# Second attention layer of a graph kernel: other rows summed by DMA, one broadcast moved ahead of a product, deeper look-ahead on VectorE

## The reference, cut to what matters

```
h = (x @ W).reshape(n, H, C)
s_src = (h * a_src).sum(-1)
s_dst = (h * a_dst).sum(-1)
e = leaky_relu(s_src[src] + s_dst[dst], 0.2)
emax = segment_max(e, dst)
ee = exp(e - emax[dst])
denom = segment_sum(ee, dst)
alpha = ee / denom[dst]
out = segment_sum(alpha[:, :, None] * h[src], dst)
```

## Time and profile before

| what | us |
|---|---|
| median of 3 executions | 968.72 |
| fastest and slowest of them | 965.46, 971.47 |
| the profiled execution | 965.46 |
| its span, first to last instruction | 963.7 |

### The profile page before, as it was taken

One profiled execution on the slowest core, in us unless ns is written; L12 is line 12 of the kernel. 1 busy time (PEld: TensorE's weight loads), 2 busy tenths in 40 slices (PEclk: granted clock), 3 DMA queues, 4 the chain that ended last, 5 costly groups with the idle time before them and its releaser, 6 DMA issues.

```text
span 963.7 us, 17472 instructions
## 1 busy us (share of the span) xinstructions
PE 915.6 (95%) x6479; PEld 674.7 (70%) x6481; DVE 746.9 (78%) x1704; ACT 364.0 (38%) x484; POOL 132.8 (14%) x154
## 2 busy tenths in 40 slices
PE   6899999989999999999999999999997799999995
PEld 5767676656665565567799999679866666666662
DVE  7978999997976889796899997899989544444443
ACT  5751212123245325324345553265447222222320
POOL 3400000000002000000000000020010344545441
PEclk9999999999999999999999999999998899999998
DMA  9611121255366486477692000169576678778860
GB/s 324 191 62 41 60 79 54 83 186 210 116 244 211 159 278 214 147 260 259 239 369 97 36 1 1 34 152 330 202 282 227 232 185 188 193 175 202 201 156 3
DMA packets 65724, 161.01 MB, mean 167 GB/s; under 512 B 15188, under 2 KB 34518, under 8 KB 62698
## 3 DMA queue, kind: packets, MB, share of 16 engines
q1 hardware_dynamic: 50282, 113.90, 33.8%
q0 software_dynamic: 10944, 38.22, 16.7%
q10 hardware_dynamic: 4416, 7.78, 2.2%
HBM read 109.13 MB, written 50.51 MB: 166 GB/s over the span
## 4 chain that ended last, share of the span: by engine, by line
PE 75%; DVE 18%; issue 3%; ACT 1%; DMA 1%; DVEq 1%; POOLq 0%; ACTq 0%; SPq 0%; POOL 0%
PE PS L2054 48%; PE PS L2353 15%; PE PS L2155 3%; DVE arena L1788 3%; PE PS L2551 2%; DVE arena L1616 2%; DVE arena L1622 1%; PE PS L2236 1%; PE PS L2166 1%; PE PS L2372 1%; DVE arena L1502 1%; PE PS L2566 1%; DVE arena L1437 1%; DVE arena L1599 1%; PE PS L2223 1%
## 5 line engine op out<-in xcount | busy, mean ns | idle before, releaser
L2054 PE MATMUL PS<-arena 128*128 128x384 f16 (+7 forms) x3396 | 560.1, 320 | 7.6 <-DVE arena L2044 3.0
L2054 PEld LDWEIGHTS PS<-arena 128*128 128x128 f16 (+2 forms) x3396 | 318.3, 98 | 210.4 <-issue 7.6
L2353 PE MATMUL PS<-arena 128*128 128x193 f32 (+1 forms) x1200 | 178.5, 310 | 3.6 <-DVE arena L1622 2.9
L2353 PEld LDWEIGHTS PS<-arena 128*128 128x128 f32 x1200 | 176.3, 191 | 5.9 <-DVE arena L1622 3.8
L1194 ACT ACTIVATE arena<-arena,AS 128x1250 f32<-128x1250 f32 x60 | 80.1, 1338 | 72.7 <-DVE arena L1616 71.2
L1622 DVE SCALAR_TENSOR_TENSOR arena<-arena 128x1250 f32<-128x1250 f32 x60 | 87.2, 1454 | 4.8 <-PE PS L2353 4.7
L1502 DVE TENSOR_SCALAR arena<-arena 128x240 f16<-128x240 f16 x324 | 88.5, 273 | 0.0
L1616 DVE SCALAR_TENSOR_TENSOR arena<-arena,AS 128x1250 f32<-128x1250 f32 x55 | 83.0, 1510 | 0.0
L1501 DVE TENSOR_SCALAR arena<-arena 128x128 f16<-128x128 f16 x324 | 79.5, 245 | 0.1
L2043 DVE SCALAR_TENSOR_TENSOR arena<-PS,arena 128x768 f32<-128x768 f32 x27 | 25.8, 957 | 62.6 <-PE PS L2054 62.6
L1326 ACT ACTIVATE arena<-PS 128x1536 f16<-128x1536 f16 x27 | 39.2, 1450 | 75.1 <-PE PS L2551 75.1
(11 more groups left out here) (280 smaller groups left out, 944.6 us busy)
## 6 DMA issues: line engine op xcount, KB each, us to landing
arena<-in_L_ffn_W_dram SPq DMA_DIRECT2D x48, 384.0 KB, 4.0
fr_d<-arena SPq DMA_DIRECT2D x48, 384.0 KB, 3.2
arena<-fr_d SPq DMA_DIRECT2D x16, 1152.0 KB, 12.3
arena<-in_x_dram SPq DMA_DIRECT2D x18, 384.0 KB, 5.5
arena<-rr_d SPq DMA_DIRECT2D x4, 1280.0 KB, 8.1
g_d<-arena SPq DMA_DIRECT2D x10, 388.0 KB, 2.5
acc_d<-arena SPq DMA_DIRECT2D x10, 384.0 KB, 2.9
xf_d<-arena ACTq DMA_DIRECT2D x10, 384.0 KB, 3.1
```

Source lines behind the costliest of these rows:

```text
L2054: m = T.matmul(out, left[i][x], right[i][y], start=first and i + r == 0, stop=last and 3 * i + r == n - 1)
L2353: m = T.matmul(ps[sum_bank(h, b)][:, r * (C + 1):(r + 1) * (C + 1)], (PT1 if deep == 3 else PT)[i % deep][:, d * P:(d + 1) * P], feats, st ...
```

## The change

Three things change in layer 2. `RELU` becomes units 0, 2, 4, 6, 8. `row(1)` on TensorE is issued straight after `row(0)`, ahead of `late_graph(2)`, and its `row_out(1)` on ScalarE ahead of `late_out(2)`. The slope steps in VectorE's loop are issued up to unit `i` + 2 for all `i`, but none at `i` = 0; before it was `i` + 1 at 0, `i` + 2 for 1 to 9, and `i` + 1 from 10 on.

```
-        RELU = (0, 2, 5, 7, 9)
+        RELU = (0, 2, 4, 6, 8)
...
                 row_out(0)
+                row_out(1)
                 late_out(2)
-                row_out(1)
                 late_out(3)
...
-                    while ahead < len(SLOPED) and SLOPED[ahead] <= i + (2 if 0 < i < NT else 1):
+                    while i and ahead < len(SLOPED) and SLOPED[ahead] <= i + 2:
                         if SLOPED[ahead] == NT:
                             dve.wait_ge(s_row_ready, 5)
                         slopes(U0 + SLOPED[ahead], *divmod(SLOPED[ahead], NT))
...
             row(0)
+            row(1)
             late_graph(2)
-            row(1)
             late_graph(3)
             row(2)
```

## The result

The changed kernel takes 972.96 us in the median of 18 executions (970.45 to 977.25); the kernel before, over 18 executions of its own, 967.05. The ratio is 1.0052 with a 95% interval of 1.004 to 1.0064: half a per cent slower, some 5.0 us (3.9 to 6.2). The two medians by themselves are 5.9 us apart, which lies inside that interval. The forecast was 972.1 us in a range of 967.5 to 977.0, with a loss of 3.4 us.

The account below looks back on a forecast made before the run. TensorE and VectorE were taken to bound layer 2 in turns, VectorE in head 1. 2.3 us from the start plus 1.1 from the tail made +3.4; 968.72 + 3.4 = 972.1 us, range 967.5 to 977.

Parts of the forecast that it names:

- Row 1 ahead of late product 2: TensorE, layer 2: row(1) stands waiting for row_out(0) from 630.4 to 632.5; first exponential 2.09 us later.
- No slope step at unit 0: Start of VectorE's loop: VectorE idles 2.7 us, row(3) waits for row_out(2), aggregation of unit 1 comes 2.9 us late.
- The other five units: Layer 2, new RELU list: summed rows land in time, units 6 and 8 wait under a microsecond; costs nothing.
- From here to the weights of unit 17 VectorE is without idle time, seven slope steps and six weights: VectorE from 672.26 to 690.55, at 1.43 us a slope step and 1.38 a weights step; unit 18 then 2.3 late.
- The tail: End of the loop: weights of unit 19 wait for the aggregation of 17, until 694.53; adds 1.1 us.
- The walk: Unit by unit timing of layer 2 on three engines; last weights start at 694.53 in place of 691.13, +3.4 us.
- The clock fell behind the standstill: Rival: TensorE's clock falls over row(1) and the late product behind it, losing about 1.6 us more; +5.0 us, chance 0.2.
- The look-ahead did not pay: Rival judged: VectorE runs without a gap from 642.50 to 691.7 instead of 692.6; -0.9 us, chance 0.12.
- The sums did not land late: Rival judged: all five summed rows in layer 2 land 5 us later; about +6.2 us, chance 0.06.
- the +5.0: Loop end 5.0 us late if TensorE's clock falls behind the new standstill; rival, chance 0.2.

Follow-up runs that it names:

- u_swap: The changed kernel with row(1) and row_out(1) put back behind late product 2; 969.27 us, ratio 1.0023 to the kernel before.
- a_first: The changed kernel with the slope step of unit 1 put back ahead of the first weights; ratio 1.003 to the kernel before, stage 88.56 us.
- u_relu: The changed kernel with RELU back at units 0, 2, 5, 7, 9; ratio 1.0043 to the kernel before.
- a_tail: The changed kernel with only the last slope step (unit 19) issued one unit later, at unit 18; ratio 1.0046 to the kernel before.
- b_fill: The kernel before with only the slope step of unit 12 issued earlier, ahead of the denominators; 965.98 us, ratio 0.9971.

## Why the prediction was right, and where its sum was short

**Sign and size.** Forecast +3.4 us; the stage gave +4.5 and the timed runs +5.0 (3.9 to 6.2), so the loss was larger than forecast, by more than the interval. That 972.1 us came so near to 972.96 is luck in part: the 968.72 it was added to, a median of three, lies 1.7 above the 967.05 of eighteen, and this made up for a loss forecast too small.

**Row 1 ahead of late product 2.** Right. A standstill of "30.4 to 632.5" measured 2.02 us, released by L1237; the shift of the first exponential, forecast 2.09, was 2.24. Alone on the old kernel 0.73 of it was regained in head 0, as was forecast for that run. In the changed kernel nothing is regained (`u_swap`: the same 59.4 behind the first exponential).

**No slope step at unit 0.** Right in mechanism: VectorE idle 2.92 for "2.7", `row(3)` held 1.48 for 1.6. The weights of unit 3, forecast at 652.65, started at 655.52 - 2.49 = 653.03 in the time of before. `a_first` prices this edit at 1.77 us.

**The other five units.** Right that their sums land in time. The prediction's "so this costs nothing" is right of the waits only: `u_relu` prices the new list at 0.50, since one slope step more falls where VectorE no longer idles. It had given the list no term of its own.

**"From here to the weights of unit 17 VectorE is without idle time, seven slope steps and six weights".** This is the term that was sized wrong. The sum took 1.38 from weights to slope step out of the rows of before, where no slope step waits for the weights just ahead. The new look-ahead makes it wait for exactly these, from unit 12 on, and then the distance is 1.49. I had named the wait (`slopes` waits for the user of its buffer) and counted only whether it would be satisfied, not that a wait on the instruction directly ahead has a price of its own. Seven steps pay it in the changed kernel: unit 12 just ahead of the quoted stretch, and units 14 to 19 in it; that of unit 13 follows the denominators. They make about 0.86 us of the 1.1 between 3.4 and 4.5. The rest, 0.26, stands in three smaller places that no run isolated: the first exponential (2.24 for 2.09), the first weights (1.44 behind it, not 1.37) and the last wait (1.26 for 1.22).

**The tail.** The last weights were released by TensorE after 1.26 us. The walk has 694.53 - 691.93 - 1.38 = 1.22 for this wait, and 1.1 net, since the last weights of before started 0.11 later than behind the pace of 1.38 (691.13 against 689.64 + 1.38). No run takes it away whole: `a_tail` cut it to 0.89. Its size rests on the timeline, where it is VectorE's only idle time in the third part.

**The rivals.** The clock fell behind the standstill in one of seven traces, at the forecast price of 1.6 us; one in seven neither supports nor contradicts a chance of 0.2. The look-ahead did not pay; it covered the 1.19 and lost more. The sums did not land late in the changed kernel. A standstill of 2.0 us was followed by a fall once, and by none six times, so the +5.0 was rightly kept as a rival and rightly not made the forecast.

## What to carry to other kernels

When two instructions on in-order engines swap places, ask what the moved one waits for and whether its cover was the thing it was moved past: here a late product hid the copy that `row(1)` needs. A deeper look-ahead helped here only where the engine waits; `b_fill` takes the one unit that covers a wait and leaves the rest, and gains, while the same depth everywhere loses. Two edits that touch one wait are not worth the same together as apart: the moved row cost 2.24 us in the changed kernel and 2.24 - 0.73 = 1.5 on the old one, where the slope step of unit 1 was made meanwhile. And a wait that is always satisfied in time still costs if it names the instruction directly ahead on the same engine, 0.12 to 0.13 us each on VectorE here, so keep the buffer's last user two steps back.

## What the runs showed of the hardware that I had not expected

- VectorE starts its next instruction ahead of the end of the last (1.37 us after the start of one that lasts 1.45). With a wait on that last one it starts 1.49 after.
- The clock of TensorE fell in every execution traced while TensorE was busy without a gap, at most 1.7 us behind the end of one of the two groups of twenty two-column products (L2394), and over a different stretch each time. In the trace of before, the second group ends at 617.76 and the clock falls between 618 and 619; the six products that follow take 3.66 us where six of the same shape just before took 2.39:

```profile
613.23 2.39 PE L2406 MATMUL PS<-arena,a2c 96*128 96x512 f32 x6
615.47 2.29 PE L2394 MATMUL PS<-a2c,arena 96*128 96x2 f32 x20
617.62 3.66 PE L2378 MATMUL PS<-arena,a2c 96*128 96x512 f32 x6
```

- The same stage up to the first exponential took 28.65, 30.33 or 31.95 us with the old row order, for the clock alone. That is more than any edit of this case costs, and it lies in the single profile. Behind the first exponential the changed kernel repeats to the hundredth whatever the clock did; the code of the kernel before regains up to 0.74 us there.
